# Weight sums spread by a TensorE product, values of the place planes on VectorE, tile 0 split inside the search, and POOL's two passes in pieces

## The reference

```python
xn = layernorm(u)
# branch 1: a state space layer; h is the running sum h[t] = lam * h[t-1] + (xn @ B_w.T)[t], lam = sigmoid(log_lambda)
y1 = h @ C_w.T + D * xn
# branch 2: a mixture of 8 experts
aff = (xn @ waff.T) / (|xn| * |waff| + 1e-9)
cap = clip(floor(512 * sigmoid(mean(aff) - threshold)), 4, 512)
keep = one_hot(argmax(softmax(aff))) * (rank of the token among the 512 by aff < cap)
y2 = sum over e of  gelu((xn * keep_e) @ W1[e] + b1[e]) @ W2[e] + b2[e]
out = u + y1 + y2
```

## Time and profile before

| | us |
|---|---|
| median of 3 runs (762.85 to 766.0) | 765.55 |
| the profiled execution | 766.07 |
| its span | 764.4 |
| TensorE busy | 600.8 (79%) |
| VectorE busy | 518.3 (68%) |
| POOL busy | 437.0 (57%) |
| ScalarE busy | 337.4 (44%) |
| mean granted clock of TensorE | 0.877 |

### The profile page before, as it was taken

How to read it: one execution, slowest core, us unless ns; L and a number is a source line. 1 busy time by engine, 2 the same in 40 slices (tenths; PEclk the granted TensorE clock), 3 DMA queues, 4 the chain that set the end, 5 groups by cost and what they waited for, 6 DMA issues and landing times.

```text
span 764.4 us, 15921 instructions
## 1 busy us (share of the span) xinstructions
PE 600.8 (79%) x4565; PEld 496.7 (65%) x4566; DVE 518.3 (68%) x985; ACT 337.4 (44%) x634; POOL 437.0 (57%) x533
## 2 busy tenths in 40 slices
PE   1865674675268616629999999999999999999995
PEld 1542342443047505629888888889889998988884
DVE  5865664651589929449977766686677667766773
ACT  3762465462249493115634444343344334433440
POOL 2842543432004683307888876777787778767643
PEclk9985767567559957869999999999999999999998
DMA  8922434573336111334522221122221121211100
GB/s 325 402 90 93 182 146 146 114 224 114 69 106 223 58 38 32 19 20 154 167 63 84 63 75 51 59 68 61 67 69 45 60 67 44 69 58 49 43 30 4
DMA packets 38191, 73.63 MB, mean 96 GB/s; under 512 B 9079, under 2 KB 23696, under 8 KB 38160
## 3 DMA queue, kind: packets, MB, share of 16 engines
q1 hardware_dynamic: 26096, 47.73, 19.4%
q0 software_dynamic: 11232, 25.20, 11.5%
q10 hardware_dynamic: 832, 0.31, 0.2%
HBM read 51.69 MB, written 27.01 MB: 103 GB/s over the span
## 4 chain that ended last, share of the span: by engine, by line
PE 54%; DMA 28%; DVE 8%; ACT 5%; issue 3%; SPq 1%; POOL 1%; ACTq 0%; DVEq 0%; POOLq 0%
DMA router_rows<-wsum 22%; PE ps_bu L842 9%; PE ps_bu L843 9%; PE ps_bu L841 9%; PE ps_t L816 4%; PE ps_t L817 4%; PE ps_t L818 4%; PE ps_y L817 4%; PE ps_y L818 4%; PE ps_y L816 4%; DMA base_rows<-area 3%; ACT work L603 2%; DVE area L1141 1%; DMA lam<-L_attn_log_lambda 1%; DMA work<-router_rows 1%
## 5 line engine op out<-in xcount | busy, mean ns | idle before, releaser
L842 PE MATMUL ps_bu<-area,ring 128*128 x624 | 170.1, 273 | 0.6 <-issue 0.4
L841 PE MATMUL ps_bu<-area,ring 128*128 x624 | 170.1, 273 | 0.5 <-issue 0.3
L843 PE MATMUL ps_bu<-area,ring 128*128 x624 | 170.1, 273 | 0.3 <-issue 0.2
L1259 DVE SCALAR_TENSOR_TENSOR ring<-ring,h_scale 128x512 f16<-128x512 f32 x156 | 117.2, 751 | 5.6
L640 ACT ACTIVATE ring<-ps_t,b1t,inv_in 128x256 f32<-128x256 f32 x156 | 79.2, 561 | 65.8 <-PE ps_t L818 55.5
L816 PE MATMUL ps_t<-work,area 128*128 128x256 f16 x312 | 86.8, 278 | 26.4 <-DVE work L1245 25.7
L467 POOL DMA_INDIRECT out<-ring,idx_b x78 | 94.9, 1216 | 19.1 <-issue 15.4
L401 POOL TENSOR_TENSOR small<-ones 128x1 f32<-128x1 f32 x156 | 48.5, 311 | 97.0 <-DVE ring L1280 40.0
L453 POOL DMA_INDIRECT work<-xn_rows,idx_x x78 | 85.0, 1090 | 26.6 <-issue 22.7
L477 POOL DMA_INDIRECT work<-base_rows,idx_b x78 | 88.6, 1135 | 18.0 <-issue 16.1
L640 ACT ACTIVATE ring<-ps_y,b1t,inv_in 128x256 f32<-128x256 f32 x156 | 78.0, 563 | 46.1 <-PE ps_y L818 20.0
(11 more groups left out here) (263 smaller groups left out, 1097.0 us busy)
## 6 DMA issues: line engine op xcount, KB each, us to landing
ring<-L_ffn_W SPq DMA_DIRECT2D x14, 1024.0 KB, 8.0
xn_rows<-area SPq DMA_DIRECT2D x8, 1024.0 KB, 11.6
base_rows<-area SPq DMA_DIRECT2D x8, 1024.0 KB, 12.8
area<-L_attn_u SPq DMA_DIRECT2D x7, 1024.0 KB, 19.2
work<-L_ffn_W SPq DMA_DIRECT2D x5, 1024.0 KB, 8.8
work<-xn_rows,idx_x POOLq DMA_INDIRECT x78
work<-base_rows,idx_b POOLq DMA_INDIRECT x78
out<-ring,idx_b POOLq DMA_INDIRECT x78
```

The source lines that it names most:

```text
L841: t.matmul(dst, hh, wh, start=(c == 0), stop=False)
L842: t.matmul(dst, hh, wl, start=False, stop=False)
L843: last = t.matmul(dst, hl, wh, start=False, stop=(c == C - 1))
L1259: v.scalar_tensor_tensor(out=hlo[p][:, cs], in0=h32[:, cs], scalar=h_scale[:, bass.ds(e, 1)], in1=hhi[p][:, cs], op0=ALU.mult, op1=ALU.sub ...
```

## The change

- The round trips of the sums through device memory are gone, and with them the helper bound on SP, `wall` and the tables. TensorE now multiplies the column of sums, spread over 128 columns as the stationary operand, with the identity: every partition gets all 128 sums in PSUM. For the 12 early units this product stands in the batch loop behind states_out, and VectorE makes the scale after the scan of that iteration instead of before it. SUMS and HIGHS name the iterations; the sums stay where they were, the scales come one iteration earlier, and the high parts of units 4, 5, 6 and 8 to 11 too.
- The four late units get four products after up(0) and one common chain of scale instructions.
- SP's queue keeps its stores and loads, without the waits of the round trips; some are moved by one or two places.
- At the start the normalisation of batches 0 and 1 no longer stands behind the constants on VectorE, TensorE and ScalarE (the exp for lambda comes after the first copies of transposed rows).
- POOL's two passes per batch are eight of 256 columns.
- POOL's product for the place planes moves to VectorE, and the second digits of the search stand after the third group of planes, not the fourth.
- ScalarE splits the rows of tile 0 within the second search, after round 11; the zero rows are copied one round later.

The diff, cut to its core:

```diff
-            def bound(n):                                             # on SP
-                sp.wait_ge(s["wsum_ok"], n + 1 if n < EARLY else UNITS)
-                sp.dma_start(bound_rows[n:n + 1, :]..., wsum[:, n:n + 1]).then_inc(s["bound_out"], 16)
-                sp.wait_ge(s["bound_out"], 16 * n + 16)
-                wait(sp, s["wscale_ok"], n - 1)
...
-                sp.dma_start(wall(n), bound_rows[n:n + 1, :]...partition_broadcast(P)).then_inc(s["bound_in"], 16)
...
+        SUMS = (1, 2, 3, 4, 6, 7, 8, 9, 10, 11, 12, 14)
+        HIGHS = (3, 4, 5, 6, 7, 8, 9, 11, 12, 13, 14, 15)
...
+                pieces = [slice(q * D, (q + 1) * D) for q in range(Q)]
+                for x in pieces:
+                    last = g.tensor_tensor(dxn[:, x], xn_(b)[:, x], d_bc[:], ALU.mult)
+                last.then_inc(s["dx_ok"], 1)
                 pool.wait_ge(s["dx_ok"], 2 * b + 1)
-                g.tensor_tensor(xu_(b), xu_(b), dxn, ALU.add).then_inc(s["dx_ok"], 1)
+                for x in pieces:
+                    last = g.tensor_tensor(xu_(b)[:, x], xu_(b)[:, x], dxn[:, x], ALU.add)
+                last.then_inc(s["dx_ok"], 1)
...
+            def bound(n, dst):                                        # on TensorE
+                return t.matmul(dst, wsum[:, n:n + 1].to_broadcast([P, P]), ident[:], start=True, stop=True)
...
+                if b - 1 in SUMS:
+                    n = SUMS.index(b - 1)
+                    pe.wait_ge(s["wsum_ok"], n + 1)
+                    pe.wait_ge(s["dve_const"], 2)
+                    wait(pe, s["wscale_ok"], n)
+                    bound(n, ps_g[:, 0:P]).then_inc(s["bound_ok"], 1)
...
+            def late_bounds():
+                pe.wait_ge(s["wsum_ok"], UNITS)
+                for n in range(EARLY, UNITS):
+                    last = bound(n, ps_bu1[:, (n - EARLY) * P:(n - EARLY + 1) * P])
+                last.then_inc(s["bound_ok"], 1)
...
             def kept_slots():
+                pe.wait_ge(s["wscale_ok"], EARLY + 1)
...
-                for n in scales.get(b, []):
-                    weight_scales(n)
                 states(b)
-                for n in lows.get(b, []):
-                    low_part(n, raw_at(n))
+                if b - 1 in SUMS:
+                    weight_scales(SUMS.index(b - 1))
+                if b - 1 in HIGHS and HIGHS.index(b - 1) < 10:
+                    low_part(HIGHS.index(b - 1), raw_at(HIGHS.index(b - 1)))
...
+                v.tensor_tensor(planes[g], planes[g], slot_val[...].to_broadcast([P, TG, NS]),
+                                ALU.mult).then_inc(s["places_ok"], 1)
...
             for g in range(4):
                 places(g)
+                if g == 2:
+                    second_digits()
...
             def second_half(n):
-                if n == 7:
+                if n == 8:
                     for i in range(E // 2):
                         zero_rows(i)
+                if n == 10:
+                    split_x(0, 0)
```

More of the change, by code:

```diff
@@ L362, in _ @@
             raw_in(15)
-            for n in range(EARLY, UNITS):
-                bound(n)
             sp.wait_ge(s["mask_ok"], 1)
@@ L561, in _ @@
             turned(0)
-            sums = {1: [0], 2: [1], 3: [2], 4: [3], 6: [4], 7: [5], 8: [6], 9: [7], 11: [8], 12: [9], 13: [10], 14: [11]}
-            highs = {3: [0], 4: [1], 5: [2], 6: [3], 8: [4], 9: [5], 10: [6], 11: [7], 13: [8], 14: [9], 15: [10]}
+            act.wait_ge(s["p_early"], 4 * 16)
+            a.activation(lam[0:N, 1:2], lam[0:N, 0:1], ACT.Exp, scale=-1.0).then_inc(s["lam_exp"], 1)
             for b in range(B):
@@ L577, in _ @@
                     a.activation(sq0, xnorm, ACT.Sqrt).then_inc(s["xroot_ok"], 1)
-                for n in highs.get(b, []):
-                    high_part(n, raw_at(n))
-                for n in sums.get(b, []):
-                    weight_sum(n)
+                if b in HIGHS:
+                    high_part(HIGHS.index(b), raw_at(HIGHS.index(b)))
+                if b in SUMS:
+                    weight_sum(SUMS.index(b))
             act.wait_ge(s["aff_ok"], 1)
@@ L664, in _ @@
             t = nc.tensor
-            pe.wait_ge(s["p_early"], 4 * 16)
             pe.wait_ge(s["consts"], 1)
-            for k in range(K):
-                t.transpose(ps_bu1[:, k * N:(k + 1) * N], st_b[:, k * P:(k + 1) * P], ident[0:N, 0:N])
-            for k in range(K):
-                t.transpose(ps_bu1[0:N, 128 + k * P:128 + (k + 1) * P], st_c[:, k, :], ident[:])
-            for k in range(K):
-                last = t.transpose(ps_bu1[:, 384 + k * E:384 + (k + 1) * E], st_w[:, k * P:(k + 1) * P], ident[0:E, 0:E])
-            last.then_inc(s["pe_const"], 1)
             def turn(b):
@@ L683, in turn @@
                     last.then_inc(s["xt_ok"], 1)
+            turn(0)
+            pe.wait_ge(s["p_early"], 4 * 16)
+            for k in range(K):
+                t.transpose(ps_bu1[:, k * N:(k + 1) * N], st_b[:, k * P:(k + 1) * P], ident[0:N, 0:N])
+            for k in range(K):
+                t.transpose(ps_bu1[0:N, 128 + k * P:128 + (k + 1) * P], st_c[:, k, :], ident[:])
+            for k in range(K):
+                last = t.transpose(ps_bu1[:, 384 + k * E:384 + (k + 1) * E], st_w[:, k * P:(k + 1) * P], ident[0:E, 0:E])
+            last.then_inc(s["pe_const"], 1)
             def states_in(b):
@@ L705, in states_out, with constants @@
                 last.then_inc(s["y_ok"], 1)
-            turn(0)
-            pe.wait_ge(s["p_late"], 4 * 16)
-            pe.wait_ge(s["dve_const"], 1)
-            t.matmul(ps_g[:, 128:128 + D], ones[0:E, :], st_b2, start=True, stop=True)
-            t.transpose(ps_g[:, 384:384 + E * C], st_b1, ident[0:E * C, 0:E * C])
-            for k in range(K):
-                last = t.matmul(ps_g[:, 0:E], ones[:], watsq[:, k * E:(k + 1) * E], start=(k == 0), stop=(k == K - 1))
-            last.then_inc(s["pe_const"], 1)
+            def constants():
+                pe.wait_ge(s["p_late"], 4 * 16)
+                t.matmul(ps_g[:, 128:128 + D], ones[0:E, :], st_b2, start=True, stop=True)
+                t.transpose(ps_g[:, 384:384 + E * C], st_b1, ident[0:E * C, 0:E * C])
+                for k in range(K):
+                    last = t.matmul(ps_g[:, 0:E], ones[:], watsq[:, k * E:(k + 1) * E], start=(k == 0), stop=(k == K - 1))
+                last.then_inc(s["pe_const"], 1)
+            def bound(n, dst):
+                return t.matmul(dst, wsum[:, n:n + 1].to_broadcast([P, P]), ident[:], start=True, stop=True)
+            pe.wait_ge(s["dve_const"], 1)
             for b in range(B):
@@ L718, in _ @@
                 states_in(b)
+                if b == 0:
+                    constants()
                 if b > 0:
@@ L855, in step @@
                 if isinstance(j, int) and j == 0:
+                    late_bounds()
                     kept_rows()
@@ L1136, in places @@
                     dve.wait_ge(s["affsum_ok"], 1)
-                v.tensor_tensor(planes[g], same(NS), of(hi16, NS), ALU.is_equal).then_inc(s["halves_ok"], 1)
+                link(v.tensor_tensor(planes[g], same(NS), of(hi16, NS), ALU.is_equal))
                 if g == 0:
@@ L1292, in step @@
                     kept_places()
-                    for n in range(EARLY, UNITS):
-                        weight_scales(n)
+                    late_scales()
                 if second:
```

123 lines of the change are left out of this document (43 added, 80 removed).

## The result

The changed kernel takes 663.84 us (median of 3 runs, 662.84 to 664.11) where the kernel before took 765.55: a ratio of 0.8677, 95% interval 0.8643 to 0.8711. The forecast was 676, in a range of 655 to 704. The profiled execution has a span of 662.1 us, 102.3 less than the 764.4 before.

What follows compares the result with a forecast made beforehand. The prediction took DMA round trips of the weight sums, holding VectorE in the batches, as the main bound. Savings of 63 + 1.5 + 6.9 + 7 + 12.5 = 90.9 us led to 676 us, range 655 to 704.

Steps and rivals of the forecast that it cites:

- The round's three instructions: Place planes before the second search, all on VectorE: 1.45, some 2.2 and 1.45 us, so 5.1 us a round.
- 90.9: Whole kernel: total forecast saving in us, 63 + 1.5 + 6.9 + 7 + 12.5, against the span of 764.4.
- stage 1: The 16 batches up to the score product, forecast at 151.3 instead of 215.06 us: 63 less, ends 36 to 83.
- the loop: Third tile's first product to the end, over 39 tiles: 425.9 us, carried over unchanged.
- the late part: Second search to third tile: 7 us less from the earlier tile 0 split, 12.5 from late sums without round trips.
- The last step of the sum: From the forecast span of 673.5 us to a measured median: 675.2, rounded up to 676.
- I take 20 us of waits: Batch loop, VectorE's waits over thirteen iterations: 20 us, 1.5 each, including 4 for high parts behind base stores.
- my 95.3 of work: Batch loop, VectorE's instructions from the add of batch 1 to the score product: 95.3 us, 7.3 per iteration.
- Rival 2: Batch loop: transfers bound it, landings of 8.0 and 12.8 us grow by half; +14, 690 us; chance 0.12.
- Rival 1: Batch loop: TensorE at its lower clock bounds it, 10.9 us an iteration against 8.9; 26 more, 702 us; chance 0.15.
- rival 5: Batch loop: the spread product waits for ScalarE's sum and holds the next transposes; +36, 712 us; chance 0.07.
- the price without them: Batch loop: if pieces did not let VectorE in, about 14 us over the stage would come back.

Runs made afterwards that it cites:

- six undone edits: Changed kernel, one edit undone each: late DMA sums 672.95 us, tile-0 split late 667.11, digits last 664.82, whole POOL passes 665.06, old opening 662.13, POOL place product 660.61.
- the kernel with the sums alone: Kernel before, with only the twelve batch-loop sums spread by a TensorE product, scales and low parts reordered to suit: 695.73 us, ratio 0.9285.

## Why the prediction was right, and where its sizes were off

**The order of the terms was right.** The round trips of the batch loop are the main part (53.3 of 88.2 us with the order that goes with them), and the late sums, the split and the digits are real and of the forecast size: 12.2, 6.3 to 6.9, and 7.0 in the comparison. The round's three instructions took 1.45, 2.29 and 1.45 us, as I had put them; the digits were ready 24.5 us after the search began, as forecast.

Of the 11.4 us by which the span fell more than 90.9, 6.5 lie in stage 1, 4.0 in the loop and 1.3 in the late part, so hardly anything made up for anything else, and 2.5 of the loop's are chance. The last step of the sum is a little off as well: with the 0.5 us between the profiled execution and the median, which it names, taken off, it makes 674.7, not 675.2.

**The waits of stage 1 were mis-sized, 20 us for 13.** The step that failed is "I take 20 us of waits". From the add of batch 1 to the score product are 108.6 us; less my 95.3 of work leaves 13.3. In the trace VectorE is busy for 98.0 of them and idle for 10.6, of which 6.9 are waits for the spread product. So the waits were half of what I took, and the work 2.7 too small. The add itself starts at 36.99, not at 36. Four of my 20 were for high parts behind base stores, because I carried over a landing of 12.8 us. Now the DMA issues of the page read:

```profile
ring<-L_ffn_W SPq DMA_DIRECT2D x14, 1024.0 KB, 6.4
xn_rows<-area SPq DMA_DIRECT2D x8, 1024.0 KB, 9.4
base_rows<-area SPq DMA_DIRECT2D x8, 1024.0 KB, 7.3
```

and no engine waits for such a store, although the stretches move 230 GB/s instead of 122. Rival 2 had the sign wrong: the landings became shorter, not longer. The round trips on SP go with the long ones: with the product alone in the kernel before, the medians of base stores and weight loads are 7.2 and 6.2 us, and with the round trips back in the changed kernel 10.7 and 7.1. By which way the trips lengthen them is open.

**The clock did not rise as I said, and it cost little.** I asked for 0.9 between 40 and 150 us; it was 0.87 from 40 to 80, 0.79 to 120 and 0.76 to 150. TensorE still waited for VectorE (10.8 us in 7 waits before the outputs), so most of what slower products take lay in its slack. VectorE was idle for 10.6 us of this stage, 6.9 of them behind the spread product, and no more than that can have come of it. Rival 1 failed not because the clock came back but because TensorE was not the bound: an iteration took 8.4 us, not 10.9.

**Two more signs failed.** The waits on sums in PSUM were to be under 1 us each; the five add up to 6.9, the longest 1.9. They are a small piece of rival 5, but not for its reason: no wait of the product for ScalarE's sum stands in the trace, the product is late because it stands behind the outputs; moved ahead of them, it left VectorE no such wait. And no wait was to be above 3 us, where ScalarE had one of 12.2 at the last scale.

**POOL's pieces** were forecast right in the small (one piece is what a VectorE instruction waits) and wrong in the price without them: 5 us, not 14, since pieces also stretch instructions that whole passes left alone. By the rule that I cited from the Trainium skill (SBUF — State Buffer, the section SBUF: two separate sides), the ports are locked for one instruction at a time; the traces agree, and show the lock in both directions: 3.53 for 1.45 on VectorE, 4.26 on POOL.

**The late part** gave 20.8 us for 19.5, but I had the wait in the wrong place. I put TensorE's wait down to the scales ahead of the slots of the kept rows. The run with late round trips shows that it waits for a low part queued behind those scales. The 5 us that I said would remain before the slots did remain (5.85), and were not needed: the down product could go first. The size came out near all the same, since the low part waits for those scales as well, by its place in VectorE's queue; my account did not have that.

**The loop** moved by 4.0 us where I had said that over 3 would prove me wrong. 1.4 of it is mine: the first step took 12.32 us before, after 15.17 us without work, at a granted clock of 0.88, and 10.92 now. Carrying over "third tile to the end" took in that slow start. The remaining 2.5 are the longer steps (6.8 us over ten steps before, 4.3 over four after). On the other chips none of the twelve executions has them, so they are no effect of the change. What they come from is open.

**What stays open.** The six undone edits, each alone, give 12.2 + 6.3 + 4.0 + 5.2 + 1.3 + 0 = 29.0 us; the changed kernel lies 34.9 below the kernel with the sums alone. The 6 us between them are not clear of the scatter: five of the six are differences of medians, and taken by their ratios, as the 5.2 is, the six come to 34.7. The stages of the traces tell more. Up to the score product the kernel with the sums alone is 8.7 us behind the changed kernel, and whole passes (5.5) and the old opening (3.2) account for that, with scatter of up to 2.8 in each. From the first search to the third tile it is 26.7 us behind, where the undone edits, each alone, give 23.2. Some 3 us there belong to edits together, 1.5 of them between the two searches: the digits' order and POOL's product cost 7.9 us in one kernel (32.4 against 24.5 from the first search to the second), and 5.1 and 1.4 apart. Nor do I know where the 16.6 us between the chips lie in the kernel before: the loop's longer steps hold 6.8, and for the rest (longer round trips would do it) there is no trace of it on another chip.

## What to carry to other kernels

Look at what is queued behind a waiting instruction before pricing the wait: with round trips no longer than before, a scale straight behind the scan cost 10.3 us each, and one with work ahead of it 6.0. So moving a consumer earlier while its latency stands may lose: here the new order and all the other edits, with the twelve round trips kept, were 1.9% slower than the kernel before. The product without the new order was not run. And when an engine idles for one input, ask whether its next work already has its own: the move of one product group gave 7 us for two lines.

## What the hardware showed that I had not expected

- Shorter POOL instructions did not simply free VectorE. Four 0.72 us pieces beside VectorE's 128x8 instructions made each of three take 0.42 to 0.57 us in the mean instead of 0.17, and halves of 512 columns were no better than whole passes (666.0 and 665.1 us).
- The same two programs stand 16.6 and 3.0 us apart on two chips. Longer steps in a steady loop, by up to 1.5 us on 10.92 and at a granted clock of 1.00, came on one of them and not on the other.
- TensorE came out of 15.17 and 11.52 us without work at a lower granted clock for about one tile (0.88 and 0.85 over the next 12 us) and lost 1.4 to 1.7 us by it.
